# A gated cross-attention and feed-forward block: narrower groups in the feed-forward, and a group's norm and quantisation between its neighbour's tiles

## What is computed

```
x = x + tanh(g_xattn) * xattn(k=ctx, v=ctx, q=layernorm(x))   # one head of 512, softmax over 722, biases bq bv bo
x = x + tanh(g_ffn) * ffn(layernorm(x))

ffn(h): h = bit_linear(h, w1)             # 512 -> 2048
        h = depthwise_conv1d(h, 3 taps over the 100 rows) + conv_b
        h = silu(h)
        return bit_linear(h, w2)          # 2048 -> 512

bit_linear(x, w): act_quant(x) @ weight_quant(w)
act_quant(x):    s = 127 / max(max|x| over the row, 1e-5);  round(x * s) clipped to int8, / s
weight_quant(w): s = 1 / max(mean|w|, 1e-5);                round(w * s) clipped to -1..1, / s
```

## Time and profile before

| | |
|---|---|
| median of 3 runs | 364.25 us (363.66 to 367.32) |
| profiled execution, its own time | 362.41 us |
| span of its profile | 360.6 us |
| PE, busy | 282.4 us (78%), 1496 matmuls |
| PEld | 202.6 us (56%) |
| DVE | 184.5 us (51%), 390 instructions |
| ACT | 154.2 us (43%), 255 |
| POOL | 99.5 us (28%), 96 |
| mean granted clock of PE | 0.886 |

### The profile page before, as it was taken

One profiled execution on the slowest core, in us unless ns is written; L12 is line 12 of the kernel. 1 busy time (PEld: TensorE's weight loads), 2 busy tenths in 40 slices (PEclk: granted clock), 3 DMA queues, 4 the chain that ended last, 5 costly groups with the idle time before them and its releaser, 6 DMA issues.

```text
span 360.6 us, 4206 instructions
## 1 busy us (share of the span) xinstructions
PE 282.4 (78%) x1496; PEld 202.6 (56%) x1496; DVE 184.5 (51%) x390; ACT 154.2 (43%) x255; POOL 99.5 (28%) x96
## 2 busy tenths in 40 slices
PE   4945999989988989658889996778978867770294
PEld 2415899756536766538668774445847734440252
DVE  0094233321225127578586445589758374896542
ACT  3002137684367552588441324298620104874000
POOL 1009000024210981133214003054403511452250
PEclk9995599999999999986999997899987596995579
DMA  6999219905696259600331500000000000000002
GB/s 197 216 228 321 87 50 301 210 3 133 154 419 160 63 122 231 146 0 3 94 72 26 140 2 0 0 3 23 25 0 0 0 0 25 0 24 23 0 2 68
DMA packets 27951, 32.19 MB, mean 89 GB/s; under 512 B 17866, under 2 KB 17866, under 8 KB 26779
## 3 DMA queue, kind: packets, MB, share of 16 engines
q1 hardware_dynamic: 27930, 31.93, 33.0%
HBM read 26.09 MB, written 1.64 MB: 77 GB/s over the span
## 4 chain that ended last, share of the span: by engine, by line
PE 22%; DVE 16%; issue 12%; ACT 6%; POOL 3%; DVEq 0%; POOLq 0%; ACTq 0%
PE pvb L591 4%; PE yb L664 3%; DVE a L1084 3%; PE ff L640 3%; DVE u L1077 2%; DVE acc_q L1089 2%; ACT z L814 2%; PE yb L461 2%; PE tr L551 2%; PE yb L626 2%; ACT ab L808 1%; PE yb L462 1%; PE yb L463 1%; PE sc L570 1%; POOL zq L875 1%
## 5 line engine op out<-in xcount | busy, mean ns | idle before, releaser
L864 POOL TENSOR_TENSOR z<-a,ab 128x300 f32<-128x300 f32 (+1 forms) x48 | 34.4, 716 | 69.3 <-DVE a L1084 69.3
L591 PE MATMUL pvb<-pt,ctx 120*128 120x100 f32 (+1 forms) x384 | 50.1, 293 | 1.8 <-ACT pt L745 1.8
L591 PEld LDWEIGHTS pvb<-pt,ctx 120*128 120x128 f32 (+1 forms) x384 | 49.0, 209 | 3.5 <-issue 3.4
L640 PE MATMUL ff<-xqt,w1t 128*128 128x300 bf16 (+1 forms) x192 | 31.9, 304 | 15.7 <-DVE u L1077 13.5
L570 PE MATMUL sc<-kt,qm 128*100 128x361 f32 x128 | 42.5, 482 | 0.0
L806 ACT ACTIVATE a<-u,convb,conv 128x300 f32<-128x300 f32 (+1 forms) x48 | 29.0, 605 | 16.0 <-DVE u L1077 15.6
L640 PEld LDWEIGHTS ff<-xqt,w1t 128*128 128x128 bf16 x192 | 18.1, 107 | 27.1 <-DVE u L1077 20.3
L551 PE MATMUL tr<-ident,ctx 120*128 120x120 f32 (+1 forms) x192 | 29.4, 276 | 4.6 <-ACT kt L724 3.1
L981 DVE COPY kt<-tr 128x361 f32<-128x361 f32 x32 | 17.0, 533 | 28.0 <-PE tr L551 25.0
L1084 DVE SCALAR_TENSOR_TENSOR a<-u,conv,a 128x297 f32<-128x297 f32 (+1 forms) x48 | 30.4, 632 | 0.9 <-ACT a L806 0.7
L551 PEld LDWEIGHTS tr<-ident,ctx 120*128 120x128 f32 (+1 forms) x192 | 23.8, 147 | 12.2 <-ACT kt L724 4.1
(11 more groups left out here) (156 smaller groups left out, 468.0 us busy)
## 6 DMA issues: line engine op xcount, KB each, us to landing
ctx<-in_ctx_dram SPq DMA_DIRECT2D x16, 720.0 KB
wraw<-in_L_ffn_w_dram SPq DMA_DIRECT2D x8, 1024.0 KB, 13.4
x_sb<-in_x_dram SPq DMA_DIRECT2D x2, 800.0 KB
out_dram<-x_sb SPq DMA_DIRECT2D x8, 200.0 KB
wq_sb<-in_L_xattn_Wq_dram SPq DMA_DIRECT2D x4, 256.0 KB, 4.2
wk_sb<-in_L_xattn_Wk_dram SPq DMA_DIRECT2D x4, 256.0 KB, 5.5
wv_sb<-in_L_xattn_Wv_dram SPq DMA_DIRECT2D x1, 1024.0 KB, 4.8
wo_sb<-in_L_xattn_Wo_dram SPq DMA_DIRECT2D x1, 1024.0 KB, 8.3
```

The source lines that it names most:

```text
L591: mm = nc.tensor.matmul(pvb[:, k * S:(k + 1) * S], cx[b % NCTX][0:r, i, k * P:(k + 1) * P], pt[0:r, i, :], start=(i == 0), stop=(i == 5))
L640: mm = nc.tensor.matmul(ffb[j % 2][:, 0:w], w1t[:, j * DK + k, :], xqt[:, k, 0:w], start=(k == 0), stop=(k == DK - 1))
L864: nc.gpsimd.tensor_tensor(z[:, q, 0:w, i].rearrange("p (b s) -> p b s", b=nb), a1[:, n % NBUF, 0:w].rearrange("p (b s) -> p b s", b=nb), a ...
```

## The change

There are five groups, of 2, 2, 2, 1 and 1 batches, so that all buffers of the feed-forward are 200 and not 300 columns wide, and new counts for the weaving. The diagonal of a group's row scales has a step of its own (`diag`), after the group's last `xi`. `row_wide` has two buffers, taken in turn by the groups; since the first broadcast now writes where raw weights still lie, the wait of DVE for the second weights' transposes stands ahead of the first copy into it and not ahead of the first tile. `fill` holds the groups 0 to 2. After batch 7's residual stand: the rest of group 2's tiles, with the norms of groups 3 and 4 and two second products among them; group 2's maximum; group 3's broadcast; group 3's tiles, with group 2's four quantisations among the first seven and then its second products; group 3's maximum; group 4's broadcast; group 4's tiles, in the same way with group 3's; group 4's maximum, quantisation, second product and store.

```diff
--- before.py
+++ after.py
@@ -32,7 +32,7 @@
 QH = B * S // 2
 CHUNK = 4
 CW = NJ * D // CHUNK
-GROUPS = [(0, 2), (2, 5), (5, 8)]
+GROUPS = [(0, 2), (2, 4), (4, 6), (6, 7), (7, 8)]
 GW = max(b1 - b0 for b0, b1 in GROUPS) * S
 NCTX = 3
 NBUF = 3
@@ -66,7 +66,7 @@
 OUT_LAG = 3
 KT_LATE = 2
 
-FILL_CUTS = [17, 22, 33, 50, 60, 77, 89, 92]
+FILL_CUTS = [17, 22, 34, 45, 61, 77, 98, 112]
 
 
 def allowed(step, out, since):
@@ -124,7 +124,7 @@
         out = [("ln2", g), ("xi", g, b0)]
         for b in range(b0 + 1, b1):
             out += [("xi", g, b), ("xqt", g, b - 1)]
-        return out + [("rbc", g), ("xqt", g, b1 - 1)]
+        return out + [("diag", g), ("rbc", g), ("xqt", g, b1 - 1)]
 
     def qz(g):
         return [("am1", g), ("am2", g)] + [("quant", g, q) for q in range(NQ)]
@@ -153,7 +153,7 @@
     fill += [("wi", 0, 2), ("m2", 2), ("wi", 0, 3), ("m2", 3), ("bvo",)]
     fill += [("wsum", 1, c) for c in range(CHUNK)] + [("wmean", 1)] + [("wi", 1, c) for c in range(CHUNK)]
     last = len(GROUPS) - 1
-    for g in range(last):
+    for g in range(last - 1):
         fill += ln2(g) + (ff_f2(g, range(*GROUPS[g - 1])) if g else ff(g)) + qz(g)
     steps += [("scores", 0, k) for k in range(DK)]
     total = len(fill)
@@ -173,11 +173,14 @@
             main += [("scores", b + 1, k) for k in range(DK)]
         weave(steps, main, fill, FILL_CUTS[b] - (total - len(fill)))
     steps += [("y", B - 1, k) for k in range(DK)] + [("xb", B - 1), ("res", B - 1)]
-    norm, second = ln2(last), list(range(*GROUPS[last - 1]))
-    steps += spread(fill, norm[:3])
-    for b in second[:TAIL_F2]:
-        steps += [("f2", last - 1, b), ("out", last - 1, b)]
-    steps += norm[3:] + ff_f2(last, second[TAIL_F2:]) + qz(last) + [("f2 all", last)]
+
+
+    i = fill.index(("quant", last - 2, 0))
+    steps += spread(fill[:i], ln2(last - 1)[:2] + ln2(last)[:2]) + ln2(last - 1)[2:]
+    steps += spread(ff_f2(last - 1, range(*GROUPS[last - 2]))[:8], fill[i:]) + ff_f2(last - 1, range(*GROUPS[last - 2]))[8:]
+    steps += qz(last - 1)[:2] + ln2(last)[2:]
+    tiles = ff_f2(last, range(*GROUPS[last - 1]))
+    steps += spread(tiles[:4], qz(last - 1)[2:]) + tiles[4:] + qz(last) + [("f2 all", last)]
     steps += [("out", last, b) for b in range(*GROUPS[last])]
     return steps
 
@@ -274,7 +277,8 @@
         acc_q = at(z_at + z_bytes + 2 * NBUF * t_bytes, "acc_q", [P, 2, GW], F32)
         acc = at(z_at + z_bytes + (2 * NBUF + 2) * t_bytes, "acc", [P, GW], F32)
 
-        row_wide = at(z_at + z_bytes + (2 * NBUF + 3) * t_bytes, "row_wide", [P, GW], F32)
+
+        row_wide = [at(z_at + z_bytes + i * t_bytes, f"row_wide{i}", [P, GW], F32) for i in (2 * NBUF + 3, 3 * NBUF + 5)]
         ab = at(z_at + z_bytes + (2 * NBUF + 4) * t_bytes, "ab", [P, NBUF, GW // S, S + 1], F32)
         wraw = at(z_at, "wraw", [P, CHUNK, CW], F32)
         w_i8 = [at(z_at + CHUNK * CW * 4, "w_i8a", [P, CW], I8), at(i8_at, "w_i8b", [P, CW], I8)]
@@ -1052,20 +1056,21 @@
                         dve.wait_ge(xq_ok, b - 1)
                     nc.vector.tensor_scalar(x_i8[:, b % 2, :], x_sb[:, b, :], mv[:, b, 0:1], row_scale[:, b:b + 1],
                                             ALU.subtract, ALU.mult).then_inc(xi_ok, 1)
-                    if b == GROUPS[step[1]][1] - 1:
-                        make_diag(step[1], row_deq)
+                elif kind == "diag":
+                    make_diag(step[1], row_deq)
                 elif kind in ("rbc", "am2"):
                     g = step[1]
                     dve.wait_ge(bc_ps, n_bc)
-                    nc.vector.tensor_copy(row_wide[:, 0:cols(g)], yb[:, 0:cols(g)]).then_inc(bcast_ok, 1)
+                    if kind == "rbc" and g == 0:
+
+                        dve.wait_ge(w2t_ok, 16 * CHUNK)
+                    nc.vector.tensor_copy(row_wide[g % 2][:, 0:cols(g)], yb[:, 0:cols(g)]).then_inc(bcast_ok, 1)
                     dve.wait_ge(bcast_ok, n_bc)
                 elif kind == "ff":
                     _, g, j = step
                     w = cols(g)
                     nb = w // S
                     if g == 0 and j == 0:
-
-                        dve.wait_ge(w2t_ok, 16 * CHUNK)
                         nc.vector.memset(ab[:, :, :, S:S + 1], 0.0)
                     if j < NJ:
                         n = NJ * g + j
@@ -1074,7 +1079,7 @@
 
                             dve.wait_ge(ab_ok, n - NBUF + 1)
                             dve.wait_ge(y1_ok, n - NBUF + 1)
-                        nc.vector.tensor_tensor(u[:, n % NBUF, 0:w], ffb[j % 2][:, 0:w], row_wide[:, 0:w],
+                        nc.vector.tensor_tensor(u[:, n % NBUF, 0:w], ffb[j % 2][:, 0:w], row_wide[g % 2][:, 0:w],
                                                 ALU.mult).then_inc(u_ok, 1)
                     if 1 <= j < NJ + 1:
                         n = NJ * g + j - 1
@@ -1119,7 +1124,7 @@
                     if n >= 2:
 
                         dve.wait_ge(hq_ok, n - 1)
-                    wide_row = row_wide[:, 0:w].unsqueeze(2).broadcast_to([P, w, QUAD])
+                    wide_row = row_wide[g % 2][:, 0:w].unsqueeze(2).broadcast_to([P, w, QUAD])
                     nc.vector.tensor_tensor(z_i8[:, n % 2, 0:w, :], z[:, q, 0:w, :], wide_row, ALU.mult).then_inc(zi_ok, 1)
                 elif kind == "out":
                     _, g, b = step
```

## The result

The changed kernel takes 411.12 us (median of 4 runs, 409.43 to 412.09) against 364.03; the ratio is 1.1424, interval 1.1313 to 1.1534. Runs of one kernel fall into faster and slower ones; a ratio compares the faster ones of both kernels, and where too few of these were left none is given. The forecast was slower, at 377 and at most 388: the sign was right, the size missed by 34 us. The profiled execution's span is 409.1 us, 48.5 more than before.

The account below looks back on a forecast made before the run. No engine was full, so order and waits bound the kernel, with latency at its end. Attention -4 and the end +17 gave +13 us, so 377 us on the scale of the runs; range 358 to 388.

Parts of the forecast that it names:

- Attention, -4 us: Batches 3 to 7, 138.6 to 293 us: 4 us shorter despite 12 more tiles and a second product; bounds -20 and +6.
- Batch 3, -4: Batch 3 gets 11 tiles, not 16, and a shorter opening burst: 4 us less.
- +3 in all: Batch 4 gets group 0's last five tiles, maximum and four quantisations, its diagonal behind a residual's chain: +3 us.
- 88 us: Batches 5 to 7 with groups 1 and 2 woven in: 88 us, against 88.5 before.
- I take 3 us off for the clock: Attention: 3 us less, as batch 7 runs at a mean clock of 0.75 and gets more matmuls around it.
- The bound of +6: Upper bound for the change in attention's time, whose expected value was -4 us.
- The end, +17: From batch 7's residual on: 85.1 us in place of 67.6, with 36 tiles for 16 and three maxima; bounds +6 and +27.
- Table loads: ScalarE: SiLU loads come to seven, Sqrt two more, Exp one more; three more in the end, 1.28 us each.
- The gaps fill: Rival, batches 5 to 7: even tiles keep PE from waiting; attention gives back 20, end grows 11, 355 us; chance 0.20.
- Small tiles are cheap: Rival, the end: pace at 100 columns proportional to width, 12 us a group, not 17.8; 366 us; chance 0.14.
- The end goes cold: Rival, the end: second products run at 1.2 GHz beside narrow tiles, +7, so 384 us; chance 0.14.
- The table rule holds: Rival, ScalarE: each table switch also costs 1.38 us of drain, 5.5 in sum, so 383 us; chance 0.04.

Follow-up runs that it names:

- e13: The kernel before with one weaving count changed, 50 to 45, so group 0's last tiles and maximum move into batch 4: 377.5 us against 363.1.
- e3: The changed kernel with no feed-forward step placed between the first y and the residual of a batch: 406.6 us, ratio 1.1265.
- e4: The changed kernel with 56 idle matmuls on PE ahead of the six longest waits of batches 4 to 6: 399.1 us, ratio 1.1089.
- e12: The changed kernel with idle matmuls ahead of waits in batches 4 to 6 and at the end: 399.8 us, no ratio.
- e6: The changed kernel with groups of 2, 2, 2 and 2 and the end as in the kernel before: 400.5 us, ratio 1.1254.
- e7: The changed kernel with the quantisations of groups 2 and 3 ahead of the next group's tiles, not between them: 412.5 us, ratio 1.1585.
- e1: The changed kernel with Copy in place of SiLU and the second norm's Sqrt, to avoid table switches: 401.2 us, ratio 1.1101.
- e2: The kernel before with Copy in place of SiLU and the second norm's Sqrt: 355.7 us, ratio 0.9881.
- e5: The changed kernel with other weaving counts, group 0's tiles ending before y of batch 3 as in the kernel before: 410.7 us, no ratio.
- e9: The changed kernel with maxima, broadcasts and quantisations of groups 0 and 1 moved among pv, and second-product steps moved: 401.6 us, ratio 1.1193.
- e10: The changed kernel with the moved steps of e9 and the 2, 2, 2, 2 groups of e6: 395.0 us, no ratio.
- e15: The kernel before with idle matmuls at waits of batches 3, 6 and 7 and the end: 353.75 us against 363.05, ratio 0.9767.

## Why the prediction was wrong, step by step

**Attention, -4 us: wrong, +24.5.** This is the step that failed. Its pieces:
- Batch 3, -4: measured -3.5, right (the same steps took 31.6 to 34.4 us in other profiles).
- Batch 4, "+3 in all": measured +13.2. I had seen that the diagonal would stand behind a residual's chain on VectorE, and priced it as waits alone, and too low. The waits in this batch are 2.4, 2.65 and 1.02 us; pv behind them is 4.9 longer than at full clock. e13 shows the same 13.1 us from one number in the kernel before.
- Batches 5 to 7, "88 us" with the group's norm, broadcasts and maximum at 8 us: measured 103. The bank `yb` was in my description and not in my sum: y of batch 5 waits 5.30 us for an addition, the second product of batch 0 4.72 for a residual. The slowness of ScalarE in the y steps, the 3 us that I did add, was not what cost (e3).
- "I take 3 us off for the clock": right for batch 7, which I named (0.75 to 0.97), and wrong in sign for the whole. I looked at the number of matmuls and not at the gaps between them; the clock of batches 4 and 6 went from 1.00 and 0.93 to 0.71 and 0.73. e4's profile gives 8 us as the clock's price in batches 5 to 7, with the waits left; the slow pv of batch 4, 4.9 us over its full rate, comes on top (an estimate: no run of that order has it fast with the waits unchanged). I had a rival for the clock, but for the end alone.
- The bound of +6 came from the waits that the trace of before held. A trace can't hold the waits of an order that it doesn't have; the row that would have given the price was there, pv of batch 7 at half clock, 9.87 us, within the window whose clock of 0.75 I cited.

**The end, +17: right in kind, +24.0.** Piece by piece, expected and measured: rest of group 2 13.8 and 16.4; norms, maximum, broadcast 7.7 and 8.4; group 3 24.2 and 24.8; between 5.0 and 5.7; group 4 20.5 and 21.8; last 13.9 and 14.5. The extrapolation to 100 columns held: two SiLUs of group 4, both ahead of its second product in the list, lie 3.2 us apart, which is the 3.2 of the line:

```profile
379.18 0.52 ACT L818 ACTIVATE z<-z 128x400 f32<-128x400 f32 x1
...
382.41 0.52 ACT L818 ACTIVATE z<-z 128x400 f32<-128x400 f32 x1
```

Each piece came out 0.6 to 2.6 us over, 6.5 in all; e12's idle matmuls took 3.0 us off the end, so part of that is the clock. The last second product, forecast at 5.5 and under 6, took 6.27. e6 confirms that one group of two is better than two of one, by 10.6 us, and e7 that the interleaving of the quantisation removes little: it shows nothing.

**Table loads** came out as counted: seven ahead of SiLU, six ahead of Exp, five ahead of Sqrt, of 1283 ns each.

```profile
L818 ACT ACT_TABLE_LOAD x7 | 9.0, 1283 | 0.1
...
L736 ACT ACT_TABLE_LOAD x6 | 7.7, 1283 | 0.1
...
L765 ACT ACT_TABLE_LOAD x5 | 6.4, 1283 | 0.1
```

e1 removed 17 loads (21.8 us) and saved 10 us of the changed kernel, e2 removed 10 (12.8 us) and saved 7 of the one before: about half of their time counts, in both.

**Rivals.** *The gaps fill* was the opposite of what happened: the even weaving opened gaps. *Small tiles are cheap* is out, by the rows above. *The end goes cold* is right in kind and too dear: the end's clock is 0.50 to 0.78, and of its five second products, of 5.34, 6.45, 3.62, 5.21 and 6.27 us, only the third ran at full rate, but e12 won 3.0 us back there, not 7. *The table rule holds* is out: the load at 349.15 is 1.28 us long and its SiLU starts at 350.44.

```profile
349.15 1.28 ACT L818 ACT_TABLE_LOAD   x1
350.44 0.54 ACT L818 ACTIVATE z<-z 128x400 f32<-128x400 f32 x1
```

The rival with the clock in attention, where e4 finds 8 us, was missing.

**The account.** Of the 48.5 us between the two profiles, 24 are in the end: 12.7 from splitting the last group (e6), and 11.3 from having the rest of group 2 with its maximum and quantisation there besides a last group of two. 24.5 are in attention. 13 of them come with the place of group 0's last tiles and maximum in batch 4 (e13), 14.5 stand in batches 5 to 7, and batch 3 gives 3.5 back. How they divide into waits, clock and added work isn't settled: e4 puts 8 us on the clock in batches 5 to 7, but in e3 pv of batches 4 and 6 ran nearly at full rate and the batches stayed almost as long, and batch 7 lost the slow pv that it had. At most some 3 us of the whole are table switches (e1, e2). What stays open is whether any order makes three groups in attention pay: e5, e9 and e10 moved the waits about and got at most 16 us back, 10 of them from the groups of e6.

## What to carry to other kernels

Where one list orders all engines, ask of each added serial chain (a maximum, its scales, a broadcast) what PE has to do beside it, and which bank its neighbours on the queue share with it. In batch 4, waits of 6.1 us in sum went with 4.9 us more in the block of matmuls behind them. Splitting a group adds such a chain, while the price of four tiles falls only from 4.6 to 3.2 us when their width is halved. And matmuls with no use, ahead of the known waits, can be worth trying: 64 of them took 9.3 us off the kernel before (e15). Where they help has to be measured, since those of batch 4 in e4 and most of those at the end in e12 brought little or nothing.
